# First loads and weight conversions of a four-layer kernel: by columns, and all issued at once

## The chip, the cores and the metric

One NeuronCore of a Trainium2 chip runs the whole kernel. The metric is the device time of one execution in microseconds; lower is better.

## What is computed

The input is `x` and `f`, each 8 batches of 512 rows and 512 columns in float32. Four layers follow one another, each with a residual:

```python
x = x + L0(x, f, seq_len1, Wq, bq, Wk, bk, Wv, bv, Wo, bo, b_prev, b_self)   # 16-head attention
x = x + L1(x, f, f, braak_embed, stage)           # softmax((x + embed) f^T) f
x = x + L2(x, language, W1, b1, W2, b2, gamma, beta)  # adapter and layer norm
x = x + L3(x, lora_language, lora_A, lora_B, lang_embed)

# inside L0, per batch
q = (f + b_self) @ Wq + bq
k = concat(x + b_prev, f + b_self) @ Wk + bk
v = concat(x, f) @ Wv + bv
score_prev = q . k[x part] * scale, masked by seq_len1
score_self = rowwise q . k[f part] * scale
weights = softmax(concat(score_prev, score_self))
out = (weights[x part] @ v[x part] + weights[self] * v[f part]) @ Wo + bo
```

## The kernel before, in words

Each engine (PE, ACT, DVE, POOL, SP) has its own program, and they meet at semaphores. float32 operands are split into two float16 parts, high and low, and each product is three matmuls (high x high, low x high, high x low); the helper `hi_lo` (L451) records them all at L458. A projection of 128 output columns over 512 rows is 12 matmuls of 512 columns, cut into 6 parts by `PARTS`, so that other steps can stand between the parts. The 512 columns of Wq and Wk make four groups g of 128 columns, which are four heads each.

The order of the work is written out by `order_mid` (L76), and every engine walks the same list and does its own share of each step. At the begin (`mid(False, True, 0)`) the list has: two transposed f tiles (`IN` 4 and 5), parts of `K` 0, `IN` 6, parts of `K` 0, `IN` 7, the rest of `K` 0, then `Q` 0, `KS` 0 (Wk on f), and for g = 1, 2, 3 `K`, `Q`, `KS`; then the V projections. Q and K are read from PSUM by ACT with their bias (L764), KS by DVE (L1043). A `HALF` step lets POOL split K or Q into float16 parts (`split`, L491, instructions L493 and L495), and after the halves of Q a group's 12 stack DMAs on SP (L624) copy them into `KQ`. From the slot `OPEN[0]` = 32 behind the start of Q 0 a score matmul of group 0 (`SMAX`, L1322) stands after each part: PE writes scores, DVE takes the maximum (L1051), ACT the exponential (L782), with two PSUM pairs in turn. The first score matmul waits for the group's 12 stack DMAs and the mask row. PSUM banks have an order of use planned by `plan_banks`; K, Q, KS alternate between banks 0 and 1, and a step waits until the user before it in its bank was read.

The begin before that list: SP loads four x tiles into `tiles_in`, then all of Wk, then each f tile into the same place as the x tile, after PE has transposed that (`load_f(-1)`, L670), then Wq. SP then waits until DVE has made the mask (`mask_made`), writes it to DRAM, loads `bo_rows`, Wv and Wo (L704 to L711). PE transposes the x tiles (`NIN` 0 to 3, L1230); ACT takes the high part (`take_high`, L735) and DVE the low part (`take_low`, L965). Weights go through a float32 stage, and ACT makes the high half (`weight_high`, L728, instruction L732) and DVE the low half (`weight_low`, L928, instruction L932), each in two instructions of 1024 elements a partition: Wk behind the x tiles, Wq behind the reading of K 0, Wv behind Q 1, Wo behind K 2 (`WEIGHTS_AT`, L142). PE waits for both halves of a whole matrix before its first use (L1252, L1254).

The biases of Q and K need the weights too, as the vectors b_prev and b_self are multiplied by them: `vector_cols` (L1208) runs 32 small matmuls a matrix on PE, and `biases_k` (L942) and `biases_q` (L954) combine them on DVE. ACT waits for `bias_done` before it reads K 0 (2) and Q 0 (3). After the bias of Q, DVE makes the mask and the row table (`mask_and_rows`, L920). POOL starts with constants and fills of `KQ` (L466 to L488), then waits for `bo_rows` (L570) before it walks the list.

The semaphore numbers count two per tile and batch (`tile_in`: x then f), and from batch 1 on both x and f go through `tiles_in` and DMA transposes; that part of the program stays.

Of the kernel before, what the change touches and what calls it, by code (L numbers as in the profile page):

```python
# [17 lines left out]
P = 128  # L18
# [123 lines left out]
WEIGHTS_AT = (("K", 0), ("Q", 1), ("K", 2))  # L142
# [98 lines left out]
def build_program(nc, x, f, len_, stage_, lang_, rlang_, Wq, bq, Wk, bk, Wv, bv, Wo, bo, b_prev, b_self,  # L241
                  embed, W1, b1, W2, b2, gamma, beta, lora_A, lora_B, lang_embed, out):
    ctx = ExitStack()
    with ctx:
# [16 lines left out]
        bias_ks = sb("bias_ks", [P, NG])  # L261
        bo_rows = sb("bo_rows", [P, D])
# [58 lines left out]
        stage32 += [x1, V]  # L321
        kpos = t1[0:B, :]
# [54 lines left out]
        W_HALVES = 2  # L377
# [86 lines left out]
        def _(eng):  # L464
# [32 lines left out]
            def mid(tail, head, i, order=None):  # L497
                b = i + 1 if tail else i
                for step in order or order_mid(tail, head):
                    if step[0] == "F16":  # L500
# [3 lines left out]
                        split(split16[:, 0, n, 0, :], split16[:, 0, n, 1, :], tiles_in[:, n, :], f_hi, n + 1, f_lo)  # L504
# [40 lines left out]
            def split_x(i):  # L545
# [4 lines left out]
                for n in range(NT):  # L550
                    eng.wait_ge(tile_in[n], b * 32 + 16)
                    split(split16[:, b % 2, n, 0, :], split16[:, b % 2, n, 1, :], tiles_in[:, n, :],
                          x_hi, i * NT + n + 1, x_lo)

            def split_f(i):
                b = i + 1
                for n in range(NT):
                    if n == 0:
                        eng.wait_ge(xt_in, i * NT * 16 + NT * 16)
                    eng.wait_ge(tile_in[n], b * 32 + 32)  # L560
# [22 lines left out]
        def _(eng):  # L583
            def load_weight(n):
                w = (Wk, Wq, Wv, Wo)[n]
                eng.dma_start(stage32[n][:, :, :], w.rearrange("(t p) n -> p t n", p=P)).then_inc(w_in[n], 16)
# [83 lines left out]
            def load_f(i):  # L670
                for n in range(NT):
                    if i < 0:
                        wait_full(eng, ("NIN", n), i)
                    else:
                        eng.wait_ge(x_lo, i * NT + n + 1)
                    load_tile(n + NT, i + 1)
# [25 lines left out]
            load_weight(0)  # L702
            load_f(-1)
            load_weight(1)  # L704
# [3 lines left out]
            for n in (2, 3):  # L708
                load_weight(n)
# [17 lines left out]
        def _(eng):  # L727
            def weight_high(n):  # L728
                eng.wait_ge(w_in[n], 16)
                for d in range(0, ND, ND // W_HALVES):  # L730
                    at = slice(d, d + ND // W_HALVES)
                    eng.activation(w_hi[:, W_ORDER[n], at, :], stage32[n][:, at, :], ACT.Copy, scale=WS  # L732
# [8 lines left out]
            def mid(tail, head, i, order=None):  # L741
                b = i + 1 if tail else i
                for step in order or order_mid(tail, head):
                    kind = step[0]
                    if kind == "IN":
                        take_high(step, b, fT)
                    elif kind in ("Q", "K"):
                        g, k = step[1], int(kind == "K")
                        wait_full(eng, step, b)
                        if not tail and g == 0:  # L750
                            eng.wait_ge(bias_done, 2 if k else 3)
# [15 lines left out]
                        if not tail and step in WEIGHTS_AT:  # L767
                            weight_high(WEIGHTS_AT.index(step) + 1)
# [113 lines left out]
            weight_high(0)  # L882
# [14 lines left out]
        def _(eng):  # L897
# [30 lines left out]
            def weight_low(n):  # L928
                for m in range(W_HALVES):
                    at = slice(m * ND // W_HALVES, (m + 1) * ND // W_HALVES)  # L930
                    eng.wait_ge(w_hi_done, W_HALVES * n + m + 1)
                    eng.scalar_tensor_tensor(out=w_lo[:, W_ORDER[n], at, :], in0=stage32[n][:, at, :], scalar=WS,  # L932
                                             in1=w_hi[:, W_ORDER[n], at, :], op0=ALU.mult, op1=ALU.subtract
                                             ).then_inc(w_lo_done, 1)

            sums = prod[:, 0:4 * NG].rearrange("p (n g) -> p n g", n=4)

            def halves(n):

                return pair[4 + 2 * n][:, 0, 0:2 * (2 - n) * NG].rearrange("p (g h v) -> p h v g", g=NG, h=2)  # L940

            def biases_k():  # L942
                of = halves(0)
                eng.wait_ge(bias_full, 1)
                eng.scalar_tensor_tensor(out=sums[:, 0, :], in0=of[:, 0, 1, :], scalar=1.0 / WS, in1=cols[:, 4:8],
                                         op0=ALU.mult, op1=ALU.add).then_inc(sums_done, 1)
                eng.scalar_tensor_tensor(out=sums[:, 1, :], in0=cols[:, 4:8], scalar=WS, in1=of[:, 0, 0, :],
                                         op0=ALU.mult, op1=ALU.add).then_inc(sums_done, 1)
                eng.wait_ge(sums_done, 2)
# [583 lines left out]
```

## Time and profile before

| | |
|---|---|
| median of 3 runs | 1336.51 us (1336.19 to 1337.59) |
| profiled execution | 1336.03 us |
| its span, first to last instruction | 1334.2 us |
| PE busy | 1271.1 us (95%) |
| DVE, ACT, POOL busy | 860.0, 847.9, 489.0 us |
| mean granted clock of PE | 0.99 |

The span is a little shorter than the execution's time, which holds what lies around it. A busy PE is not a PE at its peak, since matmuls are pipelined and their ends are modelled. In the timeline a row gives start, duration, engine, line, operation, output and input with count, and in brackets how long the engine had stood idle and what released it. A chain's row gives start, duration and what was on the chain.

### The profile page before, as it was taken

Reading aid. Unit: us, or ns where it says so; the run is one execution under the profiler, and the core shown is the slowest. Engines: PE = TensorE matmul, PEld = TensorE weight load, DVE = VectorE, ACT = ScalarE, POOL = GpSimd, SP = SyncE. Lnnn points to the kernel's source line nnn. Section 1 sums busy time; section 2 is a strip of 40 time slices with the busy share of each in tenths; the row PEclk is TensorE's granted clock in tenths of the full one; section 3 lists DMA queues with packets and bytes.
Section 4 is the critical chain, followed back from the end, with each engine's and each line's share of the span. In section 5 each row is a group of like instructions: output and inputs, shape, how many; then the busy total and the mean of one; then the engine's idle time right before and its main releaser. Section 6 shows DMA issues by size and latency. Waiting matters only on the chain.

```text
span 1334.2 us, 19509 instructions
## 1 busy us (share of the span) xinstructions
PE 1271.1 (95%) x6825; PEld 536.7 (40%) x6825; DVE 860.0 (64%) x1544; ACT 847.9 (64%) x1801; POOL 489.0 (37%) x428
## 2 busy tenths in 40 slices
PE   6999999999999999999999999999999999999995
PEld 3332454324543255333553235432454325543252
DVE  4687438864497645975379744887448864497544
ACT  3697428883398735986369753798428883398631
POOL 3434154142531427312462215614154142531114
PEclk8999999999999999999999999999999999999997
DMA  4303222133221332231331423213222034221100
GB/s 160 110 24 106 64 58 67 36 105 88 54 66 49 95 74 54 58 98 56 64 73 40 121 64 50 57 46 113 64 61 66 34 105 95 50 64 60 31 1 32
DMA packets 121295, 90.47 MB, mean 68 GB/s; under 512 B 73514, under 2 KB 94310, under 8 KB 121198
## 3 DMA queue, kind: packets, MB, share of 16 engines
q1 hardware_dynamic: 121136, 89.22, 25.9%
q8 instruction: 55, 0.90, 0.3%
q14 instruction: 42, 0.34, 0.1%
q10 hardware_dynamic: 62, 0.01, 0.0%
HBM read 40.81 MB, written 8.40 MB: 37 GB/s over the span
## 4 chain that ended last, share of the span: by engine, by line
PE 69%; DVE 15%; ACT 12%; issue 2%; DMA 1%; POOL 1%; ACTq 0%; SPq 0%; POOLq 0%; DVEq 0%
PE bank L458 27%; PE banks L458 13%; DVE nmx L1051 9%; ACT big L833 6%; PE bank L1403 6%; PE banks L1387 6%; ACT banks L782 4%; PE banks L1322 4%; PE bank L1230 4%; PE bank L1350 2%; PE bank L1355 2%; PE bank L1377 2%; PE bank L1413 1%; DVE x L1112 1%; DVE big L1108 1%
## 5 line engine op out<-in xcount | busy, mean ns | idle before, releaser
L782 ACT ACTIVATE banks<-banks,nmx 128x512 f32<-128x512 f32 x512 | 341.9, 686 | 28.1 <-DVE nmx L1051 25.8
L1051 DVE TENSOR_REDUCE nmx<-banks 128x1 f32<-128x512 f32 x512 | 329.4, 685 | 35.6 <-PE banks L1322 34.5
L833 ACT ACTIVATE big<-banks 128x1024 f32<-128x1024 f32 x256 | 247.3, 1022 | 44.2 <-PE banks L1387 43.1
L458 PE MATMUL bank<-fT,w_hi 128*128 128x512 f16 x768 | 258.4, 383 | 0.1
L1322 PE MATMUL banks<-KQ 97*128 97x512 f16 x512 | 196.6, 384 | 16.5 <-ACT banks L782 15.6
L1387 PE MATMUL banks<-KQ 98*128 98x512 f16 x512 | 141.0, 382 | 13.4 <-ACT big L833 8.4
L458 PE MATMUL bank<-fT,w_lo 128*128 128x512 f16 x384 | 146.9, 383 | 0.0
L493 POOL TENSOR_TENSOR split<-tiles_in,ones 128x512 f16<-128x512 f32 x60 | 66.0, 1100 | 219.4 <-DMA xT<-split 203.0
L493 POOL TENSOR_TENSOR half<-qk,ones 128x512 f16<-128x512 f32 x64 | 66.5, 1039 | 212.3 <-ACT qk L764 190.9
L1403 PE MATMUL bank<-big,V 128*32 128x512 f32 x1024 | 136.4, 605 | 0.0
L568 POOL TENSOR_TENSOR x<-x,bo_rows 128x512 f32<-128x512 f32 x32 | 39.7, 1273 | 237.7 <-DMA x<-in_x_dram 237.7
L782 ACT ACTIVATION_READ_ACCUMULATOR banks<-banks,nmx 128x1 f32 x512 | 118.5, 231 | 0.0
L458 PEld LDWEIGHTS bank<-fT,w_hi 128*128 128x128 f16 x768 | 75.8, 99 | 81.1 <-issue 15.4
L1322 PEld LDWEIGHTS banks<-KQ 97*128 97x128 f16 x512 | 49.2, 96 | 122.5 <-ACT banks L782 71.9
L1387 PEld LDWEIGHTS banks<-KQ 98*128 98x128 f16 x512 | 34.2, 97 | 137.7 <-ACT big L833 110.5
L458 PE MATMUL bank<-fT,q1T 128*128 128x512 f16 x384 | 88.1, 379 | 0.0
L458 PE MATMUL banks<-split,p_both 128*128 128x512 f16 x384 | 87.0, 379 | 0.0
L458 PE MATMUL bank<-xT,w_hi 128*128 128x512 f16 x256 | 83.6, 383 | 1.8 <-issue 1.8
L458 PE MATMUL bank<-w_hi,xT 128*128 128x512 f16 x256 | 82.6, 379 | 0.0
L540 POOL TENSOR_TENSOR y<-y,gr 128x512 f32<-128x512 f32 x32 | 42.7, 1334 | 97.1 <-DVE y L1014 97.1
L495 POOL TENSOR_TENSOR half<-qk,half 128x512 f16<-128x512 f32 x64 | 75.8, 1184 | 5.0
L458 PE MATMUL banks<-w_hi,xT 128*128 128x512 f16 x256 | 76.3, 380 | 0.0
(151 smaller groups left out, 1849.3 us busy)
## 6 DMA issues: line engine op xcount, KB each, us to landing
KQ<-half SPq DMA_DIRECT2D x384, 64.0 KB, 2.0
tiles_in<-in_x_dram SPq DMA_DIRECT2D x32, 256.0 KB, 7.3
tiles_in<-in_fside_BxSxS_dram SPq DMA_DIRECT2D x32, 256.0 KB, 3.7
x<-in_x_dram SPq DMA_DIRECT2D x8, 1024.0 KB, 5.9
out_dram<-x SPq DMA_DIRECT2D x32, 256.0 KB, 2.1
w<-in_L_cond_W_dram SPq DMA_DIRECT2D x16, 256.0 KB, 4.6
b2r<-in_L_cond_b_dram SPq DMA_DIRECT2D x8, 256.0 KB, 4.5
gr<-in_L_cond_gamma_dram SPq DMA_DIRECT2D x8, 256.0 KB, 5.8
```

Of the source, the lines that this page charges most:

```text
L458: mm = eng.matmul(out_ap, pairs[n][0], pairs[n][1], start=(first and n == 0), stop=(last and n == len(pairs) - 1))
L493: eng.tensor_tensor(high, src, ones[:, 0:1].to_broadcast([P, S]), ALU.mult).then_inc(high_done, 1)
L495: eng.tensor_tensor(low, src, high, ALU.subtract).then_inc(low_done, 1)
L540: eng.tensor_tensor(y[:, t % 2, :], y[:, t % 2, :], gr[:, :], ALU.mult).then_inc(scaled, 1)
L568: eng.tensor_tensor(x1[:, t, :], x1[:, t, :], bo_rows[:, :], ALU.add).then_inc(x_bo, 1)
L782: eng.activation(bank(step, i)[:, v, :], bank(step, i)[:, v, :], ACT.Exp, bias=nmx[:, t, h:h + 1], accum_out=esum[:, t, h:h + 1]).then_inc ...
L833: eng.activation(big[:, n % 2, 2 * u:2 * u + 2, :], bank(step)[:, :, :], ACT.Exp).then_inc(read(step), 1)
L1051: eng.tensor_reduce(nmx[:, t, h:h + 1], bank(step, i)[:, v, :], AX_X, ALU.max, negate=True).then_inc(max_done, 1)
L1230: mm = eng.transpose(tile_of(step, b)[:, d * P:(d + 1) * P], src[:, d * P:(d + 1) * P], ident[:, :])
L1322: eng.matmul(bank(step, i)[:, v, :], KQ[0:SHIFT_ROW, j, g, 1, t * P:(t + 1) * P], KQ[0:SHIFT_ROW, j, g, 0, :], start=True, stop=True).then ...
L1387: mm = eng.matmul(bank(step)[:, j % 2, :], KQ[0:SHIFT_ROW + 1, j, g, 0, k * P:(k + 1) * P], KQ[0:SHIFT_ROW + 1, j, g, 1, :], start=True, s ...
L1403: mm = eng.matmul(bank(("PV", g))[q, :], V[:, k, g * P + j * DH:g * P + (j + 1) * DH], big[:, n % 2, j, :], start=(k == 0), stop=(k == NT ...
```

## The change

Weights: columns of group 0 of Wk and Wq are loaded as pieces of their own (`load_weight(n, 0)`, into `w0_in`) and converted by one instruction each on ACT and DVE: Wk's behind the second x tile, Wq's behind f tile `IN` 5. The remaining 384 columns are converted at `IN` 7 (Wk) and `K` 0 (Wq). Wv and Wo stay at Q 1 and K 2, in two halves each. The f rows of batch 0 have a home of their own, `f_rows`, a float32 view of the second half of `split16`, so that the f loads wait for nothing. SP issues all its loads in one go; the mask and `bo_rows` come behind them. The small vector matmuls and the bias sums are done for group 0 first, and for groups 1 to 3 before K 1 on PE and behind the product of KS 0 on DVE. The mask and the row table move to `IN` 5 on DVE.

```diff
-WEIGHTS_AT = (("K", 0), ("Q", 1), ("K", 2))
+WEIGHTS_AT = {("IN", 5): (1, 0), ("IN", 7): (0, 1), ("K", 0): (1, 1), ("Q", 1): (2, 1), ("K", 2): (3, 1)}
+PIECES = {(0, 0): 1, (1, 0): 2, (0, 1): 4, (1, 1): 6, (2, 1): 8, (3, 1): 10}
...
+        f_rows = split16[:, 1].rearrange("p t h n -> p t (h n)").bitcast(F32)
...
             for t in range(NT):
                 load_tile(t, 0)
-            load_weight(0)
-            load_f(-1)
-            load_weight(1)
+            load_weight(0, 0)
+            for n in range(NT):
+                eng.dma_start(f_rows[:, n, :], f[0, n * P:(n + 1) * P, :]).then_inc(f0_in[n], 16)
+            load_weight(1, 0)
+            for n in range(4):
+                load_weight(n, 1)
             eng.wait_ge(mask_made, 1)
             eng.dma_start(mask_dram, mask16).then_inc(mask_out, 16)
             eng.dma_start(bo_rows[:, :], bo.rearrange("(a n) -> a n", a=1).to_broadcast([P, D])).then_inc(bo_in, 16)
-            for n in (2, 3):
-                load_weight(n)
...
+            def load_weight(n, part):
+                w, at = (Wk, Wq, Wv, Wo)[n], slice(part * P if n < 2 else 0, D if part else P)
+                eng.dma_start(stage32[n][:, :, at], w[:, at].rearrange("(t p) n -> p t n", p=P)
+                              ).then_inc(w_in[n] if part else w0_in[n], 16)
...
@@ ACT @@
+            def weight_high(n, part):
+                if part:
+                    eng.wait_ge(w_in[n], 16)
+                    for m in range(2):
+                        d, at = slice(2 * m, 2 * m + 2), slice(P if n < 2 else 0, D)
+                        eng.activation(w_hi[:, W_ORDER[n], d, at], stage32[n][:, d, at], ACT.Copy, scale=WS
+                                       ).then_inc(w_hi_done, 1)
+                else:
+                    eng.wait_ge(w0_in[n], 16)
+                    eng.activation(w_hi[:, W_ORDER[n], :, 0:P], stage32[n][:, :, 0:P], ACT.Copy, scale=WS
                                    ).then_inc(w_hi_done, 1)
...
             for n in range(NT):
                 take_high(("NIN", n), -1, xT)
-            weight_high(0)
+                if n == 1:
+                    weight_high(0, 0)
...
@@ DVE @@
                     if not tail and step in WEIGHTS_AT:
-                        n = WEIGHTS_AT.index(step) + 1
-                        if n == 1:
-                            biases_k()
-                        weight_low(n)
-                        if n == 1:
-                            biases_q()
+                        if step == ("K", 0):
+                            biases_k(0)
+                        weight_low(*WEIGHTS_AT[step])
+                        if step == ("IN", 5):
                             mask_and_rows()
+                        if step == ("K", 0):
+                            biases_q(0)
...
@@ PE @@
                     if first and step == ("K", 0):
                         eng.wait_ge(vec_lo, 1)
-                        eng.wait_ge(w_lo_done, W_HALVES)
+                        eng.wait_ge(w_lo_done, PIECES[0, 0])
                     if first and step == ("Q", 0):
-                        eng.wait_ge(w_lo_done, 2 * W_HALVES)
-                        vector_cols(1)
+                        eng.wait_ge(w_lo_done, PIECES[1, 0])
+                    if first and step == ("K", 1):
+                        eng.wait_ge(w_lo_done, PIECES[0, 1])
+                        vector_cols(0, 1)
+                        eng.wait_ge(w_lo_done, PIECES[1, 1])
+                        vector_cols(1, 1)
...
-                        if not tail and step == ("K", 0):
-                            vector_cols(0)
+                        if not tail and step in (("K", 0), ("Q", 0)):
+                            vector_cols(int(step[0] == "Q"), 0)
...
@@ DVE, behind the product of KS 0 @@
+                        if not tail and g == 0:
+                            biases_k(1)
+                            biases_q(1)
```

## Rows read from the trace of the kernel before

**Rows 1.** The head of the page.
```profile
span 1334.2 us, 19509 instructions
```

**Rows 2.** The chain of waits that ended last, stretches in order: start, duration, what.
```profile
20.76 0.16 DVE prod L945
...
21.35 0.69 ACT qk L764
...
23.02 2.37 DVE w_lo L932 x2
...
26.45 13.04 PE bank L458 x48
...
46.82 3.44 DVE w_lo L932 x2
50.26 0.61 DVE nmx L1051
...
59.06 3.01 ACT banks L782 x9
```

**Rows 3.** The timeline of PE, 10 to 52 us.
```profile
10.90 1.97 PE L1230 MATMUL bank<-ident,tiles_in 128*128 128x128 f32 x8 [0.31 <-DMA tiles_in<-in_fside_BxSxS_dram]
14.67 0.58 PE L458 MATMUL bank<-xT,w_hi 128*128 128x512 f16 x1 [1.80 <-issue]
...
19.57 0.38 PE L458 MATMUL bank<-xT,w_hi 128*128 128x512 f16 x1
...
25.43 0.27 PE L1217 MATMUL banks<-vec,w_hi 128*128 128x2 f16 x4 [4.71 <-DVE w_lo L932]
...
34.14 0.38 PE L458 MATMUL bank<-xT,w_hi 128*128 128x512 f16 x1
...
46.10 0.38 PE L1322 MATMUL banks<-KQ 97*128 97x512 f16 x1
...
51.73 0.39 PE L1322 MATMUL banks<-KQ 97*128 97x512 f16 x1 [2.51 <-ACT banks L782]
```

**Rows 4.** Stretches: us, busy time and (count) of each engine, PEclk, DMA share, GB/s.
```profile
6.00:7.00 1.00, 0.96 (x5) 0.96 (x6) 0.54 (x2) 0.00 (x0) 0.94 (x2) 1.00 0.82 268
30.00:31.00 1.00, 1.00 (x4) 0.34 (x3) 0.00 (x0) 0.00 (x0) 0.00 (x0) 0.50 0.78 211
32.00:37.00 5.00, 5.00 (x25) 2.29 (x24) 0.75 (x1) 0.38 (x2) 4.34 (x4) 1.00 0.92 351
37.00:46.00 9.00, 8.89 (x48) 3.69 (x47) 3.98 (x3) 4.04 (x6) 5.25 (x4) 1.00 0.39 94
52.00:56.00 4.00, 4.00 (x12) 1.46 (x11) 2.83 (x6) 4.00 (x12) 1.59 (x2) 0.57 0.21 51
```

**Rows 5.** The timelines of ACT and of DVE in the begin.
```profile
11.13 1.99 ACT L732 ACTIVATE w_hi<-big 128x1024 f16<-128x1024 f32 x2
...
19.12 0.60 ACT L738 ACTIVATE fT<-bank 128x512 f16<-128x512 f32 x1 [1.10 <-PE bank L1230]
...
12.21 2.36 DVE L932 SCALAR_TENSOR_TENSOR w_lo<-big,w_hi 128x1024 f16<-128x1024 f32 x2 [0.25 <-ACT w_hi L732]
...
19.75 0.69 DVE L970 TENSOR_TENSOR fT<-bank,fT 128x512 f16<-128x512 f32 x1 [1.01 <-ACT fT L738]
```

**Rows 6.** The timeline of POOL, its first and fourth halving instruction.
```profile
32.19 1.04 POOL L493 TENSOR_TENSOR half<-qk,ones 128x512 f16<-128x512 f32 x1 [18.81 <-DMA bo_rows<-in_L_cond_bo_dram]
...
35.54 1.16 POOL L495 TENSOR_TENSOR half<-qk,half 128x512 f16<-128x512 f32 x1
```

**Rows 7.** DMA issues: the stack DMAs by line; then KB each, us from issue to landing.
```profile
L624 SPq DMA_DIRECT2D KQ<-half x36: 586/597/1252, 36.7 to 63.7; - x36
...
V<-in_L_cond_Wo_dram SPq DMA_DIRECT2D x1, 1024.0 KB, 8.8
KQ<-half SPq DMA_DIRECT2D x5, 64.0 KB, 2.0
bo_rows<-in_L_cond_bo_dram SPq DMA_DIRECT2D x1, 256.0 KB, 4.1
```

More of the change, by code:

```diff
@@ L376, in build_program @@
         w_in = [sem(f"w_in{n}") for n in range(4)]
-        W_HALVES = 2
+        w0_in = [sem(f"w0_in{n}") for n in range(2)]
+        f0_in = [sem(f"f0_in{n}") for n in range(NT)]
         vec_hi = sem("vec_hi")
@@ L936, in _, with weight_low @@
[L936 to L945, printed above, removed]
+            def weight_low(n, part):
+                count = PIECES[n, part]
+                if part:
+                    for m in range(2):
+                        d, at = slice(2 * m, 2 * m + 2), slice(P if n < 2 else 0, D)
+                        eng.wait_ge(w_hi_done, count - 1 + m)
+                        eng.scalar_tensor_tensor(out=w_lo[:, W_ORDER[n], d, at], in0=stage32[n][:, d, at], scalar=WS,
+                                                 in1=w_hi[:, W_ORDER[n], d, at], op0=ALU.mult, op1=ALU.subtract
+                                                 ).then_inc(w_lo_done, 1)
+                else:
+                    eng.wait_ge(w_hi_done, count)
+                    eng.scalar_tensor_tensor(out=w_lo[:, W_ORDER[n], :, 0:P], in0=stage32[n][:, :, 0:P], scalar=WS,
+                                             in1=w_hi[:, W_ORDER[n], :, 0:P], op0=ALU.mult, op1=ALU.subtract
+                                             ).then_inc(w_lo_done, 1)
@@ new lines, in _, with halves, biases_k @@
+            sums = bias_sums[:, :].rearrange("p (n g) -> p n g", n=4)
+            def halves(n, rest):
+                return pair[4 + 2 * n][:, rest, 0:2 * (2 - n) * NG].rearrange("p (g h v) -> p h v g", g=NG, h=2)
+            def biases_k(rest):
+                of, at = halves(0, rest), slice(rest, NG if rest else 1)
+                own = slice(4 + rest, 8 if rest else 5)
+                eng.wait_ge(bias_full, 2 * rest + 1)
+                eng.scalar_tensor_tensor(out=sums[:, 0, at], in0=of[:, 0, 1, at], scalar=1.0 / WS, in1=cols[:, own],
@@ L958, in biases_q @@
+            def biases_q(rest):
+                of, at = halves(1, rest), slice(rest, NG if rest else 1)
+                own = slice(rest, 4 if rest else 1)
+                eng.wait_ge(bias_full, 2 * rest + 2)
+                eng.scalar_tensor_tensor(out=sums[:, 2, at], in0=of[:, 0, 0, at], scalar=1.0 / WS, in1=cols[:, own],
                                          op0=ALU.mult, op1=ALU.add).then_inc(sums_done, 1)
-                eng.wait_ge(sums_done, 3)
-                eng.scalar_tensor_tensor(out=sums[:, 3, :], in0=of[:, 1, 0, :], scalar=1.0 / WS, in1=sums[:, 2, :],
+                eng.wait_ge(sums_done, 4 * rest + 3)
+                eng.scalar_tensor_tensor(out=sums[:, 3, at], in0=of[:, 1, 0, at], scalar=1.0 / WS, in1=sums[:, 2, at],
@@ L1037, in mid @@
                         wait_read(eng, ("Q", g), b)
+                        if not tail and g == 1:
+                            eng.wait_ge(bias_done, 6)
                         if g >= 1:
```

67 lines of the change are left out of this document (26 added, 41 removed).

## Prediction

> **What bounds the kernel now.** I read the chain of waits first, because a begin that is shortened is worth only what its last waits are worth. From 59 us on the chain is the exponentials on ACT, back to back, and then the attention of batch 0, whose start hangs on them; what happens before 59 us is carried to the end one for one [rows 1, 2]. In the begin the chain goes: the end of K0 and its bias on DVE (20.76), K0 read by ACT (21.35), Wq converted by ACT and then DVE (23.02 + 2.37), Q0 on PE (26.45), then PE without a pause through KS0, K1, Q1, KS1 and K2 to about 45, Wo converted by ACT and DVE (46.82 + 3.44), first maximum (50.26) [rows 2]. So the first maximum is set by the end of K2, and that by the start of K1.
>
> The PE's own timeline shows what lies ahead of K1 [rows 3]: K0's first matmul at 14.67, its last at 19.57 + 0.38 = 19.95, a wait of 4.7 us for the low half of Wq before 25.43, K1's first matmul at 34.14. The view by stretches adds the clock [rows 4]: 0.50, that is 1.2 GHz, while Q0 runs (30 to 31), 1.00, that is 2.4 GHz, from 32 on; 4.7 idle us lay before the fall. At the full level a 512-column matmul follows the last after 0.216 us (12 in 2.6 us), at the half level after 0.43 (12 in 5.1 us), so the low clock costs Q0 2.5 us.
>
> **The change, part by part.** I follow K1's start through the new order.
>
> (a) The f tiles wait for no PE reading. PE waits 0.3 us before their transposes at 10.90 [rows 3]; these go to about 10.6 and end at 12.6, 1.97 us later. SP now issues its 4 + 1 + 4 + 1 + 4 loads at once, 14 issues of about half a us (the stack DMAs' 0.597 is the upper end [rows 7]), the last at 7 to 9 us; nothing that it must do earlier stands behind them.
>
> (b) K0 needs only 128 columns of Wk. Now the whole matrix is converted behind the last x tile, 2 x 1 us on ACT and 2 x 1.18 on DVE, from 12.21 [rows 5], and PE waits for it to 14.57. The new piece is 512 elements a partition, half of one of those instructions plus the fixed part: 0.6 us on ACT and 0.65 on DVE, in the gap that both have before x tile 2, while they wait for PE's transposes; without that gap it would put off x tile 2 and K0 by its 0.6 us. K0 can start right behind the f transposes, at 12.65 instead of 14.67. With its two transposes it takes 5.3 us now, partly at the slow pace; I leave that as it is: it ends at 17.95. ACT takes f tile 3 at 19.12 now [rows 5], so 17.1 then.
>
> (c) Behind f tile 3 the other 384 columns of Wk are converted before ACT may read K0. Two pieces of 768 elements: 0.8 us each on ACT (17.7 to 19.2), 0.89 each on DVE, 18.5 to 20.3. Then the bias of group 0 (four small instructions, 20.76 to 21.35 now, so 0.5 to 0.6 us), and K0 is read at 20.85 to 21.5. That is only 0.5 us before today's: the moved conversion eats most of the 2.0 us.
>
> (d) Q0 no longer waits for all of Wq. Its 128 columns are converted behind f tile 1 (13.2 to 15.2 on ACT and DVE). The mask and the row table (three small DVE instructions, an estimate of 1 us) now follow there; f tile 2 reaches DVE at about 15.8, and nothing asks for it before Q0. Q0 starts when f tile 3's low half is read, 17.1 + 0.63 + 0.69 [rows 5] = 18.45, and at the full clock ends at 21.05. The wait of 4.7 us and the low clock go.
>
> (e) What is late next is Q0's bias and reading. ACT converts the rest of Wq behind K0's reading, from 21.45; DVE 22.3 to 24.1; bias of Q0 0.55; ACT reads Q0 24.75 to 25.45. KS0 waits on PE for K0's bank until 21.5 and ends at 24.15. Then the vector columns of groups 1 to 3, which were done at once: 2 x 24 small matmuls; 32 of them fill 25.43 to about 26.3 now [rows 2, 3], so 48 take 1.3 us, on the path now, to 25.5 at the latest. K1 starts at 25.5 instead of 34.14: **8.6 us earlier**. Four and three more small DVE instructions (second halves of the biases, about 1 us) stand behind KS0's product, when DVE waits for PE; they hide under K1, and without this cover they would cost their 1 us.
>
> (f) From K1 to the first maximum nothing is edited: 11.96 us to the first score matmul at 46.10 [rows 3], and K2, Wo, the first maximum at 50.26. That gives the slot of the first score matmul at 37.5, the end of Wo's low half at 41.6.
>
> (g) One load is moved past the whole queue: bo_rows, and the mask with it, stand behind 6.3 MB. POOL waits 18.81 us for bo_rows before its first halving of K0 [rows 6], then needs 32.19 to 36.70 for K0 and Q0 (four instructions, 4.5 us), and the twelve stack DMAs of 0.597 us plus 2.0 to landing take 9.2 us more [rows 7]; that makes 45.9, and the first score matmul goes at 46.10 [rows 3], so it waits for them today already, if barely. So first score = landing of bo_rows + 13.7 us. When it lands: everything to it is 6.55 MB. Wv and Wo with full queues moved at 351 GB/s with a share of 0.92, the early Wk at 268 [rows 4]. All at 351 from about 2 us (a small DMA needs 2.0 to land, rows 7): 20.7 us. The pieces have short rows: the stack DMAs with 1 KB rows move 94 GB/s at a share of 0.39, so 241 at full share, 68 ns a packet and engine against 86 ns for 2 KB. An estimate along this line: 59 ns for 512 B, 77 ns for 1.5 KB, so the columns (0.52 MB) take 3.8 us and the rests (1.57 MB) 4.9. With x and f at 268 and the others at 351 the sum is 25.3; with all at 351 but the pieces 23.4. I take 24.3; the ends are 20.7 and 29.6 (all at 268, plus the same extra of 3.2). That first in is first out here is shown by bo_rows, which lands 4.1 us after its issue although Wv and Wo follow at once, and by Wo, 8.8 us after its own [rows 7].
> With 24.3 the first score matmul is at 38.0, half a us after its slot and 3.6 before Wo's low half: PE loses nothing that it didn't lose anyway (it waits 2.51 us before 51.73 [rows 3]). The Wk rest lands at about 16.1, wanted at 17.7; the Wq rest at 18.5, wanted at 21.5.
>
> The Trainium skill, DMA: Bandwidth & Descriptors, Specifications, says transfers reach line rate from 512 bytes up; then the pieces would cost nothing extra, bo_rows would land near 20.7, the sum would stay and rival A would lose nearly all its chance. The trace's 1 KB packets run at 241 against 381 GB/s for 2 KB (both per full share), but they go from SBUF to SBUF; I lean on the row.
>
> **The sum.** 2.0 from K0's start, minus 1.5 for Wk's rest ahead of K0's reading, 8.1 from Q0's wait, its clock and its bias: 8.6. The profiled execution took 1336.03, its span 1334.2 [rows 1], the median of the runs is 1336.51; 1336.5 - 8.6 = 1327.9, said as 1328.0. This kernel's measurement can tell 0.2% (2.7 us) from no change.
>
> **The rivals.**
> A, bo_rows too late. At 28 us the first score matmul goes at 41.8. PE then stops 4.3 us before it, and has not done the 3.1 us of work ahead (46.1 to 49.2) that it does now. It restarts at the low clock: the mean of 52 to 56 is below 1 by what about 3.4 us at 0.50 make [rows 4], a loss of 1.7 us. So the state that is reached at 51.73 + 1.7 = 53.4 now comes at 41.8 + 3.1 + 1.7 = 46.6: gain 6.8 at 28, 5.2 at 29.6, hence 1329.7 to 1331.3. For it: the 268 row. Against: 351 with full queues. Chance 0.18.
> B, the clock stays at 1.2 GHz through Q0 and KS0, as the start is shorter and broken by a wait of 0.5 us. Q0 ends at 23.6, KS0 28.8, K1 starts at 30.1: gain 4.0, 1332.5. Against: the level rose within K0 now (its first matmul is 0.58 us long, its last 0.38 [rows 3]), though PE had stood for 1.8 us before it. 0.08.
> C, slower: the column loads of 512-byte rows. If one of their packets took 200 to 260 ns an engine instead of 59, the 64 on each engine bring 9 to 13 us, bo_rows comes at 33 to 37, and by A's working the point where it decides is 35; at 37 the time is 2 us above before, 1338.5. Against: the line from 2 KB to 1 KB, which falls. 0.04.
> D, no change: Wo's conversion and the first maximum are held by something that does not move with K1, such as the halves on POOL (0.05). 1336.
> E, more: the first score matmul waits less than the 2.5 us before 51.73, or the clock doesn't fall there, which gives back up to 1.7 us: 1326.2. 0.07.
>
> **How the numbers follow.** My forecast has 0.58 (its own range 1327 to 1329.2, by 0.5 us in each of the steps b to e). With A (0.18) and E (0.07) the range 1326.2 to 1331.6 holds a bit over 0.8. Faster by over 0.2%: forecast, A, E, B = 0.91; within 0.2%: D = 0.05; slower: C = 0.04.
>
> **What would show it.** Right: K0's first matmul near 12.7, f tile 3 read by ACT near 17, K0 read near 21, Q0 from 18.5 at 0.216 us a matmul, K1 near 25.5, bo_rows landed at 22 to 27, first score near 38, first maximum near 41.7, and the whole of batch 0's attention 8.6 us earlier. Wrong: POOL's first halving after 27, a granted clock of 0.50 between 18 and 25 ACT waiting for a weight's load, or a first maximum 8.6 us earlier with an attention that is not.

## The result, and the profile after

The changed kernel takes 1326.56 us (median, 1325.3 to 1327.18), the kernel before 1336.38 us (1336.19 to 1337.59) beside it: ratio 0.9931, 95% interval [0.9918, 0.9943], so 9.2 to 9.8 us less by the ratio and by the medians. The forecast was 1328.0 (1326.2 to 1331.6). The profiled execution took 1326.49 us, its span is 1324.7 us against 1334.2 [rows 1], at a mean granted clock of 0.991.

The head of the page after:

```profile
span 1324.7 us, 19526 instructions
...
PE 1268.8 (96%) x6825; PEld 536.4 (40%) x6825; DVE 864.4 (65%) x1553; ACT 848.7 (64%) x1803; POOL 489.8 (37%) x428
```

The work is what it was, a few small instructions apart; what shrank is idle time. PE's own timeline of the changed kernel (start us, us, then the group, and in brackets the idle time before it and what ended it):

```profile
10.28 1.91 PE L1259 MATMUL bank<-ident,split 128*128 128x128 f32 x8
...
12.10 0.59 PE L465 MATMUL bank<-xT,w_hi 128*128 128x512 f16 x1
...
16.04 0.38 PE L465 MATMUL bank<-xT,w_hi 128*128 128x512 f16 x1
...
17.17 0.38 PE L465 MATMUL bank<-fT,w_hi 128*128 128x512 f16 x1 [0.57 <-DVE fT L993]
...
23.83 0.39 PE L465 MATMUL bank<-xT,w_hi 128*128 128x512 f16 x1
...
36.21 0.39 PE L1357 MATMUL banks<-KQ 97*128 97x512 f16 x1 [0.25 <-DMA KQ<-half]
...
41.98 0.39 PE L1357 MATMUL banks<-KQ 97*128 97x512 f16 x1 [2.65 <-ACT banks L795]
```

These answer to [rows 3]: K0 begins at 12.10 (before: 14.67), the 4.71 us that PE stood before Q0's small matmuls is gone (0.57 us is left, before 17.17), K1 begins at 23.83 (before: 34.14), the first score matmul goes at 36.21 (before: 46.10). The wait of 2.5 us among the score matmuls is still there, now 2.65 us before 41.98.

The chain of waits of the changed kernel through the same begin:

```profile
15.59 0.61 ACT fT L749
16.20 0.02 issue
16.22 0.70 DVE fT L993
16.92 0.25 issue
17.17 2.75 PE bank L465 x12
...
20.09 2.67 PE bank L465 x12
...
23.95 5.23 PE bank L465 x24
...
34.85 0.69 ACT qk L777
35.53 0.95 ACT w_hi L739
36.49 0.02 issue
36.51 4.00 DVE w_lo L948 x2
40.51 0.61 DVE nmx L1079
```

From Q0's first matmul to the end of K2 the chain doesn't leave PE. No conversion of Wq lies on it any more; the conversion of Wo does, and DVE needs 4.00 us for its low half where it needed 3.44 [rows 2]. The first maximum starts at 40.51 here against 50.26, 9.75 us earlier; the first exponential of batch 0's attention at 94.82 against 105.41, 10.6 us earlier.

The stretches of the changed kernel (columns as in [rows 4]):

```profile
13.00:14.00 1.00, 1.00 (x7) 0.63 (x6) 1.00 (x2) 0.35 (x1) 0.39 (x1) 1.00 1.06 372
14.00:15.00 1.00, 1.00 (x8) 0.56 (x7) 0.96 (x5) 0.60 (x1) 0.00 (x0) 1.00 1.07 384
15.00:20.00 5.00, 4.43 (x37) 2.46 (x35) 3.52 (x9) 2.80 (x5) 0.00 (x0) 1.00 1.05 386
...
42.00:44.00 2.00, 2.00 (x10) 0.63 (x10) 2.00 (x4) 2.00 (x7) 0.00 (x0) 1.00 0.42 93
44.00:46.00 2.00, 1.58 (x8) 0.51 (x8) 1.63 (x4) 2.00 (x6) 1.33 (x2) 1.00 0.21 47
```

Two things are to be seen. The loads run at 372 to 386 GB/s, while the rest of Wq, with rows of 1.5 KB, and Wv and Wo are under way. The pieces with rows of 512 bytes had landed by then, at 7.6 and 11.3 (issue plus time to landing); in the single microseconds from 5 to 11.3 the queue moved 336 to 387 GB/s, the least of it from 9 to 11. And the clock stays at 1.00 behind the 2.65 us wait, where it was 0.57 over 52 to 56 in the profile of before [rows 4].

The issues, with KB each and the time from issue to landing, and POOL's first halving:

```profile
big<-in_L_cond_Wk_dram SPq DMA_DIRECT2D x1, 768.0 KB, 7.5
big<-in_L_cond_Wq_dram SPq DMA_DIRECT2D x1, 768.0 KB, 9.1
...
big<-in_L_cond_Wk_dram SPq DMA_DIRECT2D x1, 256.0 KB, 4.9
big<-in_L_cond_Wq_dram SPq DMA_DIRECT2D x1, 256.0 KB, 5.9
bo_rows<-in_L_cond_bo_dram SPq DMA_DIRECT2D x1, 256.0 KB, 6.3
```

```profile
21.60 1.84 POOL L500 TENSOR_TENSOR half<-qk,ones 128x512 f16<-128x512 f32 x1 [8.21 <-DMA bo_rows<-in_L_cond_bo_dram]
```

bo_rows is issued at 15.12 behind the whole queue and landed 6.3 us later; POOL starts at 21.60 (32.19 before, [rows 6]).

### The profile page after: what moved, and what is told of

Its sections match the earlier page's. It is cut to its first block, busy times and chain, and to the rows that moved or that the text cites. A ratio compares the mean times of both kernels' runs of the same rounds, so it can differ in the third digit from the quotient of the medians.

```text
span 1324.7 us, 19526 instructions
## 1 busy us (share of the span) xinstructions
PE 1268.8 (96%) x6825; PEld 536.4 (40%) x6825; DVE 864.4 (65%) x1553; ACT 848.7 (64%) x1803; POOL 489.8 (37%) x428
## 4 chain that ended last, share of the span: by engine, by line
PE 69%; DVE 15%; ACT 12%; issue 2%; POOL 1%; DMA 0%; SPq 0%; ACTq 0%; POOLq 0%; DVEq 0%
PE bank L465 27%; PE banks L465 13%; DVE nmx L1079 9%; ACT big L846 6%; PE bank L1438 6%; PE banks L1422 6%; ACT banks L795 5%; PE banks L1357 4%; PE bank L1259 4%; PE bank L1385 2%; PE bank L1390 2%; PE bank L1412 2%; PE bank L1448 1%; DVE x L1140 1%; DVE big L1136 1%
## 5 line engine op out<-in xcount | busy, mean ns | idle before, releaser
L795 ACT ACTIVATE banks<-banks,nmx 128x512 f32<-128x512 f32 x512 | 342.6, 690 | 27.7 <-DVE nmx L1079 25.5
L500 POOL TENSOR_TENSOR split<-tiles_in,ones 128x512 f16<-128x512 f32 x56 | 60.5, 1080 | 220.5 <-DMA xT<-split 205.6
```

Of the source, the lines that this page charges most:

```text
L500: eng.tensor_tensor(high, src, ones[:, 0:1].to_broadcast([P, S]), ALU.mult).then_inc(high_done, 1)
L795: eng.activation(bank(step, i)[:, v, :], bank(step, i)[:, v, :], ACT.Exp, bias=nmx[:, t, h:h + 1], accum_out=esum[:, t, h:h + 1]).then_inc ...
```

## The experiments

The theory: PE no longer stands while Wq is converted, K1 comes earlier, and everything behind it keeps its distance. Rival A: bo_rows, moved behind the whole queue, sets the first score matmul. A second rival: the loads alone, issued without waits, bring the gain, and the columns nothing. Each kernel's ratio is to the kernel before on the same chip (medians of before: 1335.78, 1335.46, 1335.55 and 1334.59 us over the four sets of runs that follow).

**Loads alone.** The kernel before with the f rows in a home of their own and all loads issued at once, matrices converted whole:

```diff
-            load_f(-1)
-            load_weight(1)
+            for n in range(NT):
+                eng.dma_start(f_rows[:, n, :], f[0, n * P:(n + 1) * P, :]).then_inc(f0_in[n], 16)
+            for n in range(1, 4):
+                load_weight(n)
```

> The kernel before with half of the change: f rows in a home of their own and all loads issued at once (x, Wk, f, Wq, Wv, Wo, then mask and bo_rows); conversion by whole matrices as before. My theory (the gain is the earlier start of K1, and that comes from the columns): K0 still waits for all of Wk and starts near 14.5, Q0 still for all of Wq near 25, first maximum at 49.5 to 50.2, time 1335.5 to 1336.5. The rival (the waits of the loads, bo_rows above all, for which POOL waited 18.8 us, held the begin): POOL starts halving K0 near 22 instead of 32.2 and the first maximum comes 3 us or more earlier, 1333 or less.

Measured: 1336.02 us, ratio 1.0004 [0.9995, 1.0013]: nothing. K0 starts at 14.21 and K1 at 33.85, as before. The expectation that POOL would start near 22 missed: SP waits for the mask before it issues bo_rows, and DVE makes the mask behind Q0's bias, so:

```profile
32.28 1.04 POOL L495 TENSOR_TENSOR half<-qk,ones 128x512 f16<-128x512 f32 x1 [18.88 <-DMA bo_rows<-in_L_cond_bo_dram]
```

**Columns alone.** The changed kernel with f loaded into the input buffers again, each tile behind its wait, and mask and bo_rows ahead of Wv and Wo:

```diff
             load_weight(0, 0)
-            for n in range(NT):
-                eng.dma_start(f_rows[:, n, :], f[0, n * P:(n + 1) * P, :]).then_inc(f0_in[n], 16)
+            load_f(-1)
             load_weight(1, 0)
-            for n in range(4):
+            for n in (0, 1):
                 load_weight(n, 1)
             ...
+            for n in (2, 3):
+                load_weight(n, 1)
```

> The changed kernel without the loads' half: the f tiles are loaded behind the x tiles in the same place again, each after PE has transposed the x tile, and Wv and Wo again behind mask and bo_rows. Columns of group 0 first, as in the changed kernel. My theory: K0 starts 0.3 to 0.8 us later than in the changed kernel (12.1), K1 0.3 to 1 us later than 23.8, time 1327 to 1327.8, that is over 8.5 of the 9.8 us. The rival (both halves are needed together, as the f tiles or the rest of Wq come late): K1 after 26, 1329 or more.

Measured: 1330.31 us, ratio 0.9963 [0.9951, 0.9975]; 3 us above what was expected. The profile gives a part of it. Its timeline of ACT shows the new conversion waiting for its load, which SP issues behind the four waits for free input buffers:

```profile
14.53 0.63 ACT L747 ACTIVATE w_hi<-big 128x512 f16<-128x512 f32 x1 [1.47 <-DMA big<-in_L_cond_Wq_dram]
```

ACT's tiles f2 and f3 stand behind it; Q0 starts at 18.24 and K1 at 25.63 (17.17 and 23.83 in the changed kernel). Of these 1.8 us 1.07 are there at Q0. That execution's span was 1325.5 us, though, only 0.8 above the changed kernel's, while the medians differ by 3.7. So the same kernel ran once more:

> e2_columns_only once more, for a second profile: its profiled run was its fastest (1327.3), and its median 3 us above that. In the six kernels with a profile the attention of batch 0 starts 54.3 us after the first maximum, or 55.2 where the granted clock falls at PE's wait ahead of the fifth score matmul. My theory (its longer runs have a fall of the clock in Q 0 to K 1, as PE there has pauses of 0.95 us and more that the changed kernel lacks): median 1329 to 1331; if the profile catches one, PEclk is below 1 between 18 and 35 and K1 later than 25.6. The rival (the first six runs were chance): median 1327 to 1328.

Measured: 1330.03 us, ratio 0.9951 [0.9939, 0.9963]; the span of its profile is 1331.6, and there it was late all along: K0 at 14.49, Q0 20.47, K1 29.37, ACT waited 1.55 us for the first and 1.95 us for the second piece of its weights, and the granted clock fell to 0.50 between 28 and 34. K0's delay comes from a cast on DVE that took 3.55 us there (more on it below, at "POOL held").

**Wq's columns ahead of f.** Of the columns-alone kernel, one line moved:

```diff
-            load_f(-1)
             load_weight(1, 0)
+            load_f(-1)
```

> The kernel e2_columns_only with one load moved: Wq's first columns ahead of the f tiles instead of behind their waits. In e2_columns_only ACT waited 1.47 us for that load, and f tiles 2 and 3 were behind it. My theory (this is what columns alone lack): Q0 at 17.2 to 17.6 instead of 18.24, K1 near 24.0 to 24.8, time 2 to 3.5 us below e2_columns_only (1330.3), within 1 us of the changed kernel. The rival (Wv and Wo behind the mask, or the f tiles' waits, are what is missing): less than 1 us below e2_columns_only.

Measured: 1327.99 us (1325.5 to 1331.81), ratio 0.9946 [0.9931, 0.996]. Against the two sets of the columns alone that is 2.0 to 2.3 us less by the medians and 0.7 to 2.3 us by the ratios, and the intervals overlap. Half of the expectation came true: Q0 starts at 16.63 instead of 18.24, so the late load was what held Q0. But K1 starts at 26.12, not at 24.0 to 24.8: ACT waits 1.44 us for the rest of Wk, PE stands 1.47 us before KS0, and the low half of Wq's rest takes DVE 3.10 us, with POOL beside it:

```profile
21.15 1.04 POOL L500 TENSOR_TENSOR half<-qk,ones 128x512 f16<-128x512 f32 x1 [7.78 <-ACT qk L781]
...
21.73 3.10 DVE L952 SCALAR_TENSOR_TENSOR w_lo<-big,w_hi 128x768 f16<-128x768 f32 x2 [1.55 <-ACT w_hi L743]
```

In the two profiles of the changed kernel POOL starts 0.9 and 1.8 us after that pair has begun, and the pair takes 1.82 and 1.83 us. In the three profiles with the loads in the old manner POOL starts 0.6 us before the pair (twice) or 0.8 us after its begin, and the pair takes 2.69 to 3.10 us. So a part of what the columns alone lack, about 1 us at K1, is this meeting of POOL and DVE. How the deficit splits between it and the late loads is not shown.

**bo_rows late.** The changed kernel with two more loads of 1 MB (Wo into a buffer that is free then; nothing is computed from them) ahead of the mask's wait and bo_rows:

```diff
+            for n in range(2):
+                if n:
+                    eng.wait_ge(extra_in, 16 * n)
+                eng.dma_start(p1_both[:].rearrange("p a b n -> p (a b) n"), Wo.rearrange("(t p) n -> p t n", p=P)
+                              ).then_inc(extra_in, 16)
```

> The changed kernel with two more loads of 1 MB (Wo into a place not yet in use, one after the other) ahead of mask and bo_rows. bo_rows should land near 28.8 instead of 21.5. My theory (first score matmul = landing of bo_rows + 13.7 to 14.8 us, harmless up to about 26, as Wo's low half ends at 40.5): first score matmul near 42.7 instead of 36.2, PE without its work ahead, first maximum near 43.1, time 1330 to 1333. The rival (bo_rows has slack, another wait sets the first score matmul): 1326.5, no change.

Measured: 1332.29 us, ratio 0.9973 [0.9962, 0.9984]. POOL starts at 30.28 and the first score matmul goes 13.8 us later, as rival A had it. PE's timeline:

```profile
33.41 0.61 PE L466 MATMUL bank<-fT,w_hi 128*128 128x512 f16 x1 [4.86 <-ACT qk L784]
...
44.06 0.39 PE L1364 MATMUL banks<-KQ 97*128 97x512 f16 x1 [1.67 <-DMA KQ<-half]
```

Most of the wait falls at another place than A put it: ACT can't read K1 before POOL has halved K0, so PE stops before Q1. From there the chain runs through K2 and Wo's low half to the first maximum (46.44), not through the first score matmul. The time is near A's (1331.3 at 29.6 us), but the price is not: 5.7 us above the changed kernel, where A had 3.4 above its forecast. So a late bo_rows does cost, by a longer path than A's; the condition for it doesn't hold in the change, where POOL starts 8.7 us sooner.

**bo_rows early.** Its load ahead of Wv and Wo instead of behind them:

```diff
             for n in range(4):
+                if n == 2:
+                    eng.dma_start(bo_rows[:, :], bo.rearrange("(a n) -> a n", a=1).to_broadcast([P, D])).then_inc(bo_in, 16)
                 load_weight(n, 1)
```

> The changed kernel with bo_rows loaded ahead of Wv and Wo instead of behind the mask. POOL may start halving when K 0 is read (19.9) instead of 21.6, and the stack DMAs end about 0.5 to 1 us earlier. My theory (the first maximum hangs on Wo's low half, not on this): first score matmul near 35.8, first maximum at 40.4 as before, time within 0.5 us of the changed kernel. The rival (bo_rows still bounds): 1 us faster or more.

The changed kernel ran beside it, on the same chip:

> The changed kernel once more, unedited, beside the kernel before on one chip. Every theory: a ratio of 0.992 to 0.994. In its profile the start of K1 near 23.8 and a PE wait of about 2.6 us ahead of the fifth score matmul; my theory of the spread of the times (that wait ends sometimes with a fall of the granted clock, as before, and sometimes without): runs some 1 to 3 us apart, the longer ones with the lower mean clock. The rival (the changed kernel never falls there, which is part of its gain): all its runs at a clock of 0.991 or more.

Measured: 1326.68 us, ratio 0.9941 [0.9928, 0.9954], against 1326.32 us, 0.9931 [0.9918, 0.9945]. Nothing is gained, though POOL starts 1.8 us sooner; the first score matmul goes at 36.79 instead of near 35.8. The timeline says what POOL meets:

```profile
19.84 1.04 POOL L500 TENSOR_TENSOR half<-qk,ones 128x512 f16<-128x512 f32 x1 [6.46 <-ACT qk L778]
...
20.43 3.10 DVE L949 SCALAR_TENSOR_TENSOR w_lo<-big,w_hi 128x768 f16<-128x768 f32 x2 [1.55 <-ACT w_hi L740]
```

Wq's low half takes DVE 3.10 us beside POOL; in the changed kernel the same pair starts first, at 20.71, and takes 1.82 us, and it is POOL's instruction that is lengthened (1.84 instead of 1.04). K1 starts at 24.82, 1.0 us later. The first maximum is only 0.3 us later (40.74), as Wo's low half takes 3.32 us there instead of 4.00.

In the second profile of the changed kernel K1 starts at 23.35, PE again waits 2.65 us before the fifth score matmul, and here the clock falls behind it (rows further below). Its mean granted clock is 0.993, above the 0.991 of the first profile, which has no fall. So the mean clock of a run doesn't tell whether the fall was in it, and neither the theory nor its rival is decided by the list of runs.

**Wo converted sooner.** ACT converts Wv behind Q0 and Wo behind K1 (in the change: behind Q1 and K2), DVE Wv behind K1 and Wo behind Q1:

```diff
-WEIGHTS_AT = {("IN", 5): (1, 0), ("IN", 7): (0, 1), ("K", 0): (1, 1), ("Q", 1): (2, 1), ("K", 2): (3, 1)}
+WEIGHTS_AT = {("IN", 5): (1, 0), ("IN", 7): (0, 1), ("K", 0): (1, 1), ("Q", 0): (2, 1), ("K", 1): (3, 1)}
+LOW_AT = {("IN", 5): (1, 0), ("IN", 7): (0, 1), ("K", 0): (1, 1), ("K", 1): (2, 1), ("Q", 1): (3, 1)}
```

> The changed kernel with Wv and Wo converted earlier, as they have been in SBUF since about 21: ACT makes Wv's high half behind the reading of Q 0 and Wo's behind K 1, DVE the low halves at K 1 and Q 1, instead of at Q 1 and K 2. My theory (the first maximum at 40.4 hangs on Wo's low half, and all behind it moves with it): the first maximum follows the first score matmul at 36.2 to 36.6, near 37, and the time falls by 3 to 4 us to 1322.5 to 1323.5. The rival (PE, which then has no work ahead, or the stack DMAs become the bound soon after): the first maximum is early but the time falls by less than 1.5 us.

Measured: 1323.51 us, ratio 0.9911 [0.9896, 0.9925], some 3 us below the changed kernel. So the first maximum hung on Wo's low half, as the chain says; rival D's kind of hold doesn't act. The bound behind it is the stack DMAs:

```profile
28.82 4.15 DVE L949 SCALAR_TENSOR_TENSOR w_lo<-V,w_hi 128x1024 f16<-128x1024 f32 x2
...
37.12 0.39 PE L1358 MATMUL banks<-KQ 97*128 97x512 f16 x1 [1.73 <-DMA KQ<-half]
...
37.55 2.65 DVE L1080 TENSOR_REDUCE nmx<-banks 128x1 f32<-128x512 f32 x4 [3.92 <-PE banks L1358]
```

**Both.** With POOL's chain now the bound, the earlier bo_rows was tried again on top:

> Both edits of e4_wo_early and e5_bo_early. In e4_wo_early the first score matmul waited 1.73 us for the stack DMAs, so bo_rows bounds there. My theory: the first score matmul at 35.3 to 36.3 instead of 37.1, and the time 0.7 to 1.5 us below e4_wo_early, about 1322 to 1322.8 (0.990 of the kernel before). The rival (POOL's halving of Q 0, which waits for Q 0's reading at 23.5 and runs beside DVE, sets the stack alone): same time as e4_wo_early.

Measured: 1323.74 us, ratio 0.9913 [0.99, 0.9926], the same as Wo sooner alone. POOL's lead is spent on DVE in part: the pair at 20.25 takes 3.10 us, K1 starts at 24.64 instead of 23.55. Yet the first score matmul no longer waits for the stack DMAs (36.32 instead of 37.12), the first maximum comes 0.8 us sooner (36.74 against 37.55), and so does the attention (91.42 against 92.24). The expected gain is there in the begin. The rest of the span, 1230.5 against 1229.3 us, takes it back in the two profiles; why isn't known, and a gain of 0.8 us lies within the intervals.

**POOL held.** The kernel of both edits, POOL waiting for Wq's low half before its first halving:

```diff
             eng.wait_ge(bo_in, 16)
+            eng.wait_ge(w_lo_done, PIECES[1, 1])
```

> e6_both with one wait more: POOL's first halving waits until DVE has made the low half of Wq's rest. In e5_bo_early and e6_both POOL's first halving (from 19.7 to 19.8) ran beside that instruction pair, which took 3.10 us instead of 1.83, and K1 started at 24.6 to 24.8 instead of 23.4 to 23.8. My theory (the two slow each other, and that is why the earlier bo_rows brought nothing): the pair takes 1.83 again, K1 starts near 23.6, POOL starts near 22.1; first score matmul 36.2 to 37.0, time within 0.7 us of e6_both (1323.7). The rival (the pair is slow for another reason, such as the loads then in flight): it stays at 3.10 and K1 at 24.6, time 1 us or more above e6_both.

Measured: 1326.05 us (1323.33 to 1329.38), ratio 0.9918 [0.9903, 0.9933]. The time missed. That the two slow each other is borne out: in its profile the pair takes 1.83 us again, and from Q0's to K1's start 6.67 us pass, as in the changed kernel (6.66), against 7.94 with POOL beside it. That this is why the earlier bo_rows brought nothing is not: from Q0's start to the first maximum 20.8 us pass here and 20.0 in the kernel of both edits, as the stack DMAs are late now (PE waits 1.86 us for them before the first score matmul). What the wait gives back at K1 it takes at the stack. And all of it lies 6 us later, for another reason:

```profile
7.10 6.31 DVE L929 CAST vec<-cols 128x8 f16<-128x8 f32 x1
...
9.87 3.51 POOL L496 MEMSET KQ<- 32x4096 f32 x1
...
26.63 1.83 DVE L951 SCALAR_TENSOR_TENSOR w_lo<-big,w_hi 128x768 f16<-128x768 f32 x2 [1.55 <-ACT w_hi L742]
...
28.70 1.04 POOL L501 TENSOR_TENSOR half<-qk,ones 128x512 f16<-128x512 f32 x1 [15.32 <-DVE w_lo L951]
```

An 8-column cast on DVE takes 6.31 us: it began at 7.10, while POOL filled the mask rows (fills at 6.42 and 9.87, 3.51 us each), and it ended at 13.41, when the second fill did (13.38). In the second profile of the columns alone it is 3.55 us long, from 6.44 to 9.99; in the eleven profiles in which it began by 6.36, it took 0.17 to 0.58 us. Six of these eleven began between 5.81 and 6.14 and all ended at 6.39 to 6.41, just after POOL's IOTA did (5.82 to 6.38): the same wait, with a short instruction. So a vector that lands 0.1 to 0.7 us later than usual stops DVE, and everything behind it, for one or two fills.

**Mask early in the kernel before.** Is the wait of 18.8 us for bo_rows [rows 6] worth anything by itself? The mask, the row table and with them bo_rows moved up to f tile 1, nothing else of the change:

```diff
+                        if step[1] == NT + 1:
+                            mask_and_rows()
...
-                            mask_and_rows()
```

> The kernel before with one part of the change: DVE makes the mask and the row table behind f tile 1 instead of behind the bias of Q. SP's wait for the mask ends near 16 instead of 27.6, so bo_rows, Wv and Wo are loaded 11 us earlier, and POOL's wait of 18.8 us for bo_rows shrinks to about 8. My theory (that wait was covered; the first maximum hangs on K1, K2 and Wo): POOL halves K 0 near 21.6, first score matmul at 46 as before, since its slot on PE comes no sooner, first maximum at 50.2, time as before within 0.7 us. The rival (bo_rows was part of the bound): 2 us faster or more.

Measured: 1338.25 us, ratio 1.0019 [1.0009, 1.003]: 2.5 us slower, outside what was expected. POOL's wait was idle time that cost nothing, and it kept POOL away from DVE; now they meet (POOL's next instruction, at 23.70, takes 2.01 us):

```profile
22.58 1.04 POOL L493 TENSOR_TENSOR half<-qk,ones 128x512 f16<-128x512 f32 x1 [9.16 <-ACT qk L764]
...
23.38 3.41 DVE L932 SCALAR_TENSOR_TENSOR w_lo<-big,w_hi 128x1024 f16<-128x1024 f32 x2 [1.76 <-ACT w_hi L732]
```

2.37 us before [rows 2], 3.41 us now, and K1 at 35.47 instead of 34.14. The first maximum and the attention start 1.2 and 1.3 us later. So the meeting of the two accounts for about half of the 2.5 us; the rest lies behind the attention's start in this profile and stays open.

**Fills held.** The kernel with Wo sooner, POOL's fills waiting until DVE has cast the vectors:

```diff
             eng.wait_ge(sel_ready, 2 + 2 * NG)
+            eng.wait_ge(vec_lo, 1)
```

> e4_wo_early with one wait more: POOL's two fills of KQ (3.51 us each, from 6.42 on) wait until DVE has made vec16 (two tiny instructions). In eleven profiles DVE's cast of vec16 took 0.17 to 0.58 us where it began by 6.36, and in the two where it began at 6.44 and 7.10, with the fills running, it took 3.55 and 6.31 and ended when a fill ended; all that follows moved by as much. My theory (an execution whose small vectors land late loses 3 to 6 us to the fills, part of the spread of all these kernels): the cast below 0.6 us, fills from 6.5 to 7.5 on, nobody waits for them, median 1322 to 1323.7 and all runs within 2 us. The rival (the long casts had another cause): a spread of 3 us or more as in e8_pool_held (1323.3 to 1329.4), median at e4_wo_early's 1323.5 or above.

Measured: 1323.24 us (1321.71 to 1324.58), ratio 0.9903 [0.9883, 0.9922]. The spread, 2.9 us, is wider than expected and no proof of anything; the profile shows the order that the wait enforces:

```profile
6.49 0.17 DVE L928 CAST vec<-cols 128x8 f16<-128x8 f32 x1
...
6.98 3.51 POOL L496 MEMSET KQ<- 32x4096 f32 x1 [0.62 <-DVE vec L930]
```

The cast began at 6.49, later than the 6.44 at which it had taken 3.55 us, and took 0.17. The kernel is 3 to 4 us faster than the change and 11.4 (by the ratio 13) below before, the shortest time of all; against Wo sooner alone (0.9911) the intervals overlap, so a gain by the held fills is not shown.

## Why the prediction was right, and where it wasn't

The forecast's path is the one that happened, step for step; the gain was 1.2 us larger by the medians. That it came out so near is in part luck: at the attention of batch 0 the forecast was 2.0 us too low (8.6 against 10.6), and the rest of the span, which it took to be carried one for one, took 1.1 us back.

(a) f's transposes: predicted 10.6 to 12.6, measured 10.28 to 12.1.

(b) The largest miss. K0 was left at today's length of 5.3 us; it took 4.32, taken the same way (12.10 to 16.04 + 0.38). Its matmuls follow each other after about 0.43 us up to about 13.5 and after 0.216 from there, 1.4 us after K0's first one; before, the pace stayed at 0.43 for 3.4 us, to about 18. That is the pace of the half level, but the column of the granted clock reads 1.00 over these stretches in both profiles, so that the clock is the reason is not shown by it. In the kernel before PE stood 1.80 us ahead of K0, now the f transposes run right up to it. Nor is that shown to be the cause: in the second profile of the changed kernel K0 has the full pace from its first matmul (3.46 us from there to the next group), but with the mask early in the kernel before PE stood 2.06 us ahead of K0, and K0 began at the full pace and fell to 0.43 after 0.9 us. With the start 0.55 us sooner than predicted, ACT takes f tile 3 at 15.59 instead of 17.1, and that 1.5 us runs through every later step.

(c) The rest of Wk cost what was said: 0.79 us a piece on ACT, 0.92 on DVE, and it stands ahead of K0's reading, which came at 19.26 (predicted 20.85, before 21.35).

(d), (e) Q0 started at 17.17 (18.45) and ran at the full clock; its bias and the rest of Wq held its reading to 23.08 (24.75); K1 started at 23.83 (25.5). The timelines of ACT and DVE, with both pairs of rests:

```profile
16.08 1.57 ACT L739 ACTIVATE w_hi<-big 128x768 f16<-128x768 f32 x2
...
23.08 0.69 ACT L777 ACTIVATE qk<-bank,bias_q 128x512 f32<-128x512 f32 x1 [1.67 <-DVE bias_q L986]
```

```profile
16.95 1.83 DVE L948 SCALAR_TENSOR_TENSOR w_lo<-big,w_hi 128x768 f16<-128x768 f32 x2
...
20.71 1.82 DVE L948 SCALAR_TENSOR_TENSOR w_lo<-big,w_hi 128x768 f16<-128x768 f32 x2 [1.55 <-ACT w_hi L739]
```

The 48 small matmuls took 1.2 us on the path (1.3 predicted), from 22.61 to 23.83. The second halves of the biases hide, at 24.56 to 25.7.

(f) "Nothing is edited" was 0.5 us off. From K1's start to the first score matmul 12.4 us passed (11.96 before), and Wo's low half took 4.00 us instead of 3.44. POOL's halves lie beside it in both; before, the first of them began 0.8 us ahead of DVE's pair (46.04 and 46.82), now 0.2 us (36.30 and 36.51), so DVE waits for nearly all of it. So the first maximum came 9.75 us earlier, less than K1's 10.3.

(g) bo_rows was priced too dear: 24.3 forecast, 21.4 measured. The sum leaned on the 1 KB rows of the stack DMAs and gave the short rows 2.7 us extra (23.4 minus 20.7; the 3.2 that the text adds at its upper end is another sum, and is too high by 0.5). Little of that showed: the queue moved 336 to 387 GB/s from 5 us on, and only the two microseconds from 9 to 11 were below 340, which is worth some 0.3 us against 387. The Trainium skill (DMA: Bandwidth & Descriptors, Specifications: line rate from 512 bytes up) was weighed there and set aside; by it bo_rows lands near 20.7, and the trace, with 21.4, is nearer to it than to my row. It cost the sum nothing, since bo_rows hides either way, but it is why rival A had 0.18 and C 0.04. The distance from landing to the first score matmul was priced too low: 14.8 us (21.4 to 36.21) instead of 13.7, as POOL's four instructions took 5.3 us beside DVE instead of 4.5; PE waited 0.25 us for the stack DMAs, which 1.1 us less would have hidden. The stack DMAs go from SBUF to SBUF: the row was of another kind of transfer.

Rival E's part did happen in the profiled execution: the clock stayed at 1.00 behind the wait of 2.65 us. The second profile of the same kernel has the fall:

```profile
42.00:44.00 2.00, 2.00 (x8) 0.75 (x7) 2.00 (x4) 2.00 (x8) 0.00 (x0) 0.70 0.44 98
44.00:46.00 2.00, 2.00 (x7) 0.63 (x6) 1.05 (x2) 2.00 (x8) 1.74 (x2) 0.50 0.01 4
```

Of the ten profiles with Wo at its old place, five without a fall need 54.33 to 54.38 us from the first maximum to the attention, five with one (that of before among them) 55.23 to 55.30. The fall costs 0.9 us, not the 1.7 that the text took from [rows 4] (in A's price too). Without a fall the chain behind the wait is ACT's exponentials, back to back; with one it runs through PE's matmuls for 4 to 5 us, and only what these take beyond the exponentials is lost.

The working then closes: 10.3 at K1, minus 0.56 for Wo, 0.9 for the clock, makes the 10.6 us at the attention. The rest of the span takes 1229.9 us against 1228.8; over all profiles it lies between 1228.0 and 1230.5 without an order that follows the edits, and what it is stays open. So does why the columns alone are as uneven as they are: two profiles show a good and a bad execution, not how often either comes.

The two parts of the change are not a sum. The loads alone bring 0 and the columns alone 5 to 6.5 us, together 9.2 to 9.8: while K0 waits for the conversion of the whole Wk, f and Wq may land as early as they like; once conversions are small, the load is the next to be late. The new order of loads also moves bo_rows back, and so keeps POOL off DVE's pair at 20.7, by little: in the profile with the fills held, where DVE is 0.5 us later, they meet and the pair takes 2.67 us. The prediction saw only a risk in the late bo_rows.

## What to carry to other kernels

Split a preparation (here a weight's conversion) so that only what the first product needs stands ahead of it, and then look at when each piece's load is issued: earlier loads alone gave nothing here, and the split alone gave half to two thirds. An engine that waits off the path may be doing its neighbour a favour; before a wait of POOL's is taken away, look at what DVE runs at that time. To price a transfer take a row of the same kind, HBM to SBUF or SBUF to SBUF, and not the one nearest in row length.

## What the runs showed of the hardware

- DVE and POOL slow each other when both read SBUF: pairs of scalar_tensor_tensor with two SBUF inputs went from 1.83 to 3.10 us (768 elements) and from 2.36 to between 3.2 and 4.15 (1024), and POOL's tensor_tensor from 1.04 to 1.84 and from 1.16 to 2.02. The Trainium skill (SBUF — State Buffer, Who interferes with whom) has this rule: a DVE instruction with two SBUF inputs and a GpSimd instruction that reads SBUF exclude each other, the second waits for the first. The runs agree, and the held POOL gave the 1.83 us back.
- A running fill on POOL stops a tiny fp32 to fp16 cast on DVE to the fill's end: 3.55 and 6.31 us instead of 0.17 to 0.58, in the two profiles in which they met. A tenth of a us decides: a cast that began at 6.36 took 0.17 us. A tensor_tensor of the same 8 columns, begun at 6.43 with a fill running from 6.42, took 0.17 as well.
- A deep queue of loads with rows of 1.5 KB and 2 KB moves 372 to 386 GB/s, at a share of 1.05 to 1.07, against 351 at 0.92 [rows 4] in the kernel before. While pieces of 256 KB with rows of 512 bytes were among the loads, it moved 336 to 387.
- The same wait of PE, 2.4 to 2.65 us, is followed by 1.2 GHz in some executions of a kernel and not in others (5 of those 10 profiles), at 0.9 us each time.
